# Layer 1 of a four-layer fused kernel: the order of work inside a step, the place of the next sample's gather, and the expert biases

## The reference, cut to what matters

```python
xn = _layernorm(x, axis=-1)
# s: causal scores of 32-wide queries and keys, softmax, values
V = inputs @ (Wvdown @ Wvup);  s = softmax(masked(Q @ K.T / sqrt(32))) @ V
# g: 8 experts of 128x128, top 1 by the router
logits = xt @ router_w + router_b;  probs = softmax(logits)
gate = max(probs);  idx = argmax(probs)
out_all = einsum('th,ehd->ted', xt, expert_w) + expert_b[None]
y = gate * out_all[t, idx];  x = x + s * silu(y)
```

## Time and profile before

| what | us |
|---|---|
| median of 3 runs | 1436.09 (1435.06 to 1437.58) |
| the profiled execution | 1434.19 |
| its span, first to last instruction | 1432.4 |
| layer 0, ends at | 573.3 of the span |
| layer 1 | 573.3 to 732.8 |
| layers 2 and 3 | 732.8 to 1432.4 |
| PE / DVE / ACT / POOL busy over the span | 82 / 70 / 53 / 42 % |

### The profile page before, as it was taken

How to read it: one execution, slowest core, us unless ns; L and a number is a source line. 1 busy time by engine, 2 the same in 40 slices (tenths; PEclk the granted TensorE clock), 3 DMA queues, 4 the chain that set the end, 5 groups by cost and what they waited for, 6 DMA issues and landing times. The chain is left out here.

```text
span 1432.4 us, 21079 instructions
## 1 busy us (share of the span) xinstructions
PE 1169.7 (82%) x7042; PEld 828.3 (58%) x7042; DVE 999.9 (70%) x2279; ACT 762.1 (53%) x1579; POOL 606.8 (42%) x601
## 2 busy tenths in 40 slices
PE   3999999998888694687876887888887874899995
PEld 1455655664554483476653554656555653678885
DVE  2476677679787464567646988989889896714555
ACT  1456556555445354344436685676677472426553
POOL 3243445444358633533101532724633543315772
PEclk9999999999999897688878998898899797779997
DMA  7300000000000122800000000000000000001113
GB/s 179 109 1 1 1 1 1 1 2 1 1 13 24 57 86 74 268 11 15 1 12 0 1 1 1 1 1 0 1 1 1 0 1 0 30 8 34 45 42 107
DMA packets 54456, 40.72 MB, mean 28 GB/s; under 512 B 13191, under 2 KB 46701, under 8 KB 54349
## 3 DMA queue, kind: packets, MB, share of 16 engines
q1 hardware_dynamic: 41006, 27.58, 6.6%
q0 software_dynamic: 4544, 9.32, 2.3%
q10 hardware_dynamic: 8800, 2.48, 0.9%
HBM read 26.32 MB, written 13.04 MB: 27 GB/s over the span
## 5 line engine op out<-in xcount | busy, mean ns | idle before, releaser
L780 POOL TENSOR_TENSOR PR<-PR,R 128x512 f32<-128x512 f32 (+3 forms) x128 | 160.5, 1266 | 230.3 <-DVE R L1260 229.8
L1978 POOL TENSOR_TENSOR YY<-YY,H 128x512 f32<-128x512 f32 x120 | 162.3, 1375 | 206.3 <-DVE H L2349 206.3
L410 PE MATMUL banks<-XT,we 128*128 128x128 f32 (+1 forms) x568 | 178.1, 445 | 11.2 <-ACT HH L2196 10.8
L1067 ACT ACTIVATE PR<-banks,NM 128x257 f32<-128x257 f32 (+3 forms) x256 | 132.4, 527 | 99.3 <-DVE NM L1232 97.5
L410 PEld LDWEIGHTS banks<-we,HH 128*128 128x128 f32 x1024 | 147.5, 208 | 36.6 <-issue 32.1
L2341 DVE TENSOR_TENSOR_SCAN H<-DA,H 128x1024 f32<-128x1024 f32 x64 | 164.6, 2572 | 0.4 <-DVE OH L466 0.3
L410 PE MATMUL banks<-we,HH 128*128 128x128 f32 x1024 | 147.5, 292 | 0.0
L2196 ACT ACTIVATE HH<-banks,be1f 128x512 f32<-128x512 f32 x128 | 84.1, 686 | 93.1 <-PE banks L410 92.4
L410 PEld LDWEIGHTS banks<-XT,we 128*128 128x128 f32 x568 | 91.2, 203 | 65.3 <-issue 44.2
L410 PE MATMUL banks<-BCR,SEL 96*128 96x512 f32 x128 | 68.9, 540 | 72.5 <-DVE H L2349 61.2
L410 PEld LDWEIGHTS banks<-PTS,V 128*64 128x64 f32 x1152 | 65.9, 138 | 86.0 <-issue 50.2
(11 more groups left out here) (535 smaller groups left out, 2461.1 us busy)
## 6 DMA issues: line engine op xcount, KB each, us to landing
xsort<-zrow SPq DMA_DIRECT2D x1, 3072.0 KB, 13.8
XS<-xsort SPq DMA_DIRECT2D x12, 256.0 KB, 3.0
ysort<-PTS SPq DMA_DIRECT2D x12, 256.0 KB, 2.2
pj_stage<-in_L_ffn_w_proj SPq DMA_DIRECT2D x1, 2048.0 KB, 11.9
we<-in_L_ffn_we SPq DMA_DIRECT2D x1, 2048.0 KB, 15.1
we<-yrows SPq DMA_DIRECT2D x8, 256.0 KB, 4.5
xrows<-XN SPq DMA_DIRECT2D x4, 256.0 KB, 2.3
out<-XN SPq DMA_DIRECT2D x4, 256.0 KB, 2.3
```

Of the source, the lines that this page charges most:

```text
L410: return nc.tensor.matmul(o, l, r, start=start, stop=stop)
L780: last = nc.gpsimd.tensor_tensor(p, p, R[:, T * q + t, :].unsqueeze(2).to_broadcast([P, 2, w]), ALU.mult)
L1067: nc.scalar.activation(PR0[:, q % 2, s, OFF[t]:OFF[t] + w], ps2(n)[:, s, SLOT[t]:SLOT[t] + w], ACT.Exp, bias=NM[:, m, s:s + 1], accum_out= ...
L1978: nc.gpsimd.tensor_tensor(YY[:, m, :], YY[:, m, :] if n else XD[m], H[:, k % 4, m, :], ALU.add).then_inc(ya, 1)
```

## The change

1. **The biases are folded.** Two small loads put the 8 bias rows of layer 1's experts into partition 0 of XN and SA, which are free during layer 0. In three free slots of the spare bank in layer 0's last sample (u = 9, 10, 11) PE forms the column sums of the expert weights less the bias, and of the query, key, value and router weights; DVE subtracts a 128th part of them from the weights. In layer 1 ACT stores the features with 1 added. As normed rows sum to zero, features plus one times the new weights is the old product plus bias. The weights transpose, its store, the bias products and `store_bias` go, and the first expert is written into ACC by a multiplication instead of added.
2. **The steps are turned round.** Sample j + 1 is weighed after the last row maximum of step j, its gate is stored and its norm statistics are taken after expert 5, its norm applied between experts 6 and 7. A step therefore begins on PE with the features of sample j, then expert 0, transposes 0, queries and keys, logits, expert 1, and so on. ACT's order follows.
3. **Gathers a step ahead.** POOL issues the gathers of sample j + 2 at the end of step j, behind the inverse deviation of sample j + 1.

```diff
-                    return ("sel",) if u == 8 else None
+                    return {8: ("sel",), 9: ("e1", 0), 10: ("e1", 1), 11: ("q1",)}.get(u)
...
+                            elif kind == "e1":
+                                pe.wait_ge(s_late, 16)
+                                mm(o, ones[:, :], EW[:, 4 * b:4 * b + 4, :].rearrange("p e d -> p (e d)"), start=True, stop=False)
+                                last = mm(o, minus[0:1, :], (XN, SA)[b][0:1, :, :].rearrange("p t d -> p (t d)"), start=False, stop=True)
+                            elif kind == "q1":
+                                for i, w in enumerate((wqp, wkp, wv1, Wr1)):
+                                    last = mm(o[:, i * P:i * P + w.shape[1]], ones[:, :], w[:, :])
...
+                                w = EW[:, 4 * b:4 * b + 4, :].rearrange("p e d -> p (e d)")
+                                nc.vector.scalar_tensor_tensor(w, o, -1.0 / P, w, ALU.mult, ALU.add).then_inc(m7, 1)
...
POOL, layer 1
+                        scales(0)
+                        gather_rows(g, 1, YG, s_back[1])
+                        for j in range(B):
                             for t in range(T):
                                 g.wait_ge(fi, T * j + t + 1)
                                 nc.gpsimd.tensor_tensor(SC[:, j % 2, t, :], SC[:, j % 2, t, :], FI[:, t % 2, :], ALU.add).then_inc(fd, 1)
+                            if j + 1 < B:
+                                scales(j + 1)
+                            if j + 2 < B:
+                                g.wait_ge(ya, j + 1)
+                                gather_rows(g, j + 2, YG, s_back[j + 2])
...
ACT
-                            nc.scalar.activation(XT[:, j % 2, :], PS[:, 0, :], ACT.Copy).then_inc(xts, 1)
+                            nc.scalar.activation(XT[:, j % 2, :], PS[:, 0, :], ACT.Identity, bias=ones[:, 0:1]).then_inc(xts, 1)
```

More of the change, by code:

```diff
@@ L1524, in expert @@
                             last.then_inc(yp, 1)
[L1526 to L1534, removed]
-                        def biases(b):
-                            pe.wait_ge(wTs, b + 1)
-                            weighted_biases(0, NE, Eb).then_inc(bi, 1)
                         def transposes(b, t):
@@ L1579, in _ @@
                             front, back, more = j < B, j > 0, j + 1 < B
+                            if front:
+                                features(j)
                             if back:
-                                weights(b)
                                 expert(b, 0)
+                                transposes(b, 0)
+                            if front:
+                                queries_keys(j)
+                                logits(j)
+                            if back:
                                 expert(b, 1)
                                 turn(TURNS[j][0:1])
-                                transposes(b, 0)
-                                biases(b)
                                 transposes(b, 1)
                             if front:
-                                features(j)
+                                scores(j, 0)
+                                scores(j, 1)
                             if back:
@@ L1593, in _ @@
                                 values(b, 1)
-                                turn(TURNS[j][1:2])
                             if front:
-                                queries_keys(j)
-                                logits(j)
+                                v_rows(j)
+                                scores(j, 2)
                             if back:
                                 expert(b, 3)
+                                turn(TURNS[j][1:2])
                                 transposes(b, 2)
@@ L1602, in _ @@
                             if front:
-                                scores(j, 0)
-                                scores(j, 1)
+                                scores(j, 3)
+                            if more:
+                                choices(j + 1)
                             if back:
@@ L1608, in _ @@
                                 values(b, 2)
-                                values(b, 3)
-                            if front:
-                                v_rows(j)
-                                scores(j, 2)
-                            if back:
-                                expert(b, 5)
-                            if more:
-                                choices(j + 1)
-                            if front:
-                                scores(j, 3)
-                            if back:
-                                expert(b, 6)
-                                turn(TURNS[j][3:4])
                             if more:
@@ L1624, in _ @@
                             if back:
+                                values(b, 3)
+                                expert(b, 5)
+                                turn(TURNS[j][3:4])
+                                expert(b, 6)
+                                turn(TURNS[j][4:])
                                 expert(b, 7)
-                                turn(TURNS[j][4:])
                     @block.scalar
@@ L1833, in _ @@
                             if front:
[L1834 removed]
+                                router(j)
                             if back:
                                 add_expert(b, 1)
[L1837 to L1841 removed]
                             if front:
@@ L1863, in _ @@
                             if back:
-                                add_expert(b, 7)
+                                add_expert(b, 4)
+                                add_expert(b, 5)
                             if more:
                                 finish_next(j + 1)
+                                stats_in(j + 1)
+                            if front:
+                                choose(j)
                             if back:
+                                add_expert(b, 6)
+                            if more:
+                                apply_in(j + 1)
+                            if back:
+                                add_expert(b, 7)
                                 finish(b)
```

102 lines of the change are left out of this document (45 added, 57 removed).

## The result

The changed kernel takes **1415.5 us** (median of 4 runs, 1412.72 to 1425.31) where the kernel before took 1435.8 on the same chip (4 runs, 1435.06 to 1437.58): a ratio of 0.9866, 95% interval 0.9836 to 0.9895. The forecast was 1425.4 with a range from 1417 to 1433, so the gain of 20 us is nearly twice the 10.7 forecast. On a second chip the ratio was 0.9872 (0.9843 to 0.9901), 18.6 us of 1451.9, so the size is no accident of one chip.

A forecast was written before the change was run, and what follows sets the result against it. A chain from engine to engine was taken to bound layer 1's steps, with bias waits and PE's low clock. From 1434.19 us, -11.4 + 0.7 gave 1423.5; with 1.9 for the median, 1425.4, range 1417 to 1433.

The forecast's parts named there:

- Layer 1: The new order and folding end this layer at 721.4 us instead of 732.8, 11.4 us earlier.
- The middle step: Layer 1, from one sample's features to the next: 34.3 us by a walk of the new order, against 37.5 before.
- DVE's waits: In a middle step of layer 1 they sum to 6.2 us, against 10.4 before, with none for ACC.
- Rival (a): Layer 1's PE pause is only moved and DVE's waits stay at 10.4 us: 9.6 us lost, 1435.0 us; chance 0.10.
- Layer 0: The folding's added PE and DVE work in the last sample, mostly covered by POOL's queue: +0.7 us, bounds 0 and 7.4.
- Rival (c): The folding costs its full 7.4 us in layer 0, reads holding up key and query products: 1432.1 us; chance 0.11.
- The gathers: Layer 1's gathers, issued a step ahead on POOL, end before the first fill with 3.2 us slack: 0, bounds 0 and 2.
- The clock in layer 1: PE runs at half clock for the first 5.6 us of a step, after idling over 5 us.
- rival (b): Half clock lasts through the head of layer 1's steps: 4.6 us more in each of steps 1 to 3, 1439.2; chance 0.07.
- Rival (d): Layer 1's waits for scores 3 and the silu shrink: steps of 31.5 us, 1417 us in all; chance 0.08.
- the sum: Whole kernel: -11.4 us for layer 1 and +0.7 for layer 0 give -10.7; no term for layers 2 and 3.
- the signs that the prediction named as proof against it: Steps longer than 36 us, a second fall of the clock, or fills that wait for gathers.

The follow-up runs named there:

- experiment 1: The kernel before with only the biases folded, ratio 0.9941, or only the new step order, ratio 0.9953.
- experiment 2: The changed kernel without its three folding jobs in layer 0's last sample: ratio 0.9903, layer 0 ending at 576.35 us.
- experiment 3: The changed kernel with useless PE products behind expert 7 in layer 1: six 0.9919, eight 0.9921, eight in steps 1 and 2 only 0.9892.
- experiment 5: DVE multiplications added at layer 1's end: changed kernel with 3, 8, 16: 0.9911, 0.9956, 0.9983; kernel before with 16: 1.0061.
- experiment 6: Useless PE products in layer 2's pauses: two everywhere, changed kernel 0.9931, before 0.9991; chosen places, before 0.9906, changed with layer 1's products 0.9834.
- experiment 4: Both kernels run again unchanged on a second chip: changed kernel 0.9872, kernel before against itself 0.9986.

## Why the prediction missed

**Layer 1: right.** Features at 603.11, 637.78 and 672.22 us, forecast 603.35, 637.65 and 671.95; the end at 720.5, forecast 721.4. The middle step, forecast as 34.3 us, took 34.4 to 34.7. Of DVE's waits, forecast as 6.2 us (gate 0.7, logits 2.1, scores 1.9, silu 1.5), 7.2 were measured: 0.7, 1.9, 2.4 and 1.8, and 0.4 for an expert that the forecast had without a wait. The gain of 11.8 us, 12.6 on the second chip, stands against a forecast of 11.4. The last stretch was 1.1 us shorter than forecast (48.3, not 49.4). Over all profiles the kernel before took 157.5 us for this layer on the mean of five, the changed code 146.0 on the mean of eight without products in it: 11.5 us. Rival (a) is out: the pause has indeed stayed (7.09 us), but the waits have shrunk.

**The parts.** The prediction priced a middle step with both parts only, and that price was right. Taken apart, the folding frees the first step (3.1 to 5.1 us); what it does alone in a middle step is not shown (experiment 1).

**Layer 0: right in kind.** Forecast +0.7 us, measured -0.45 and -0.9, with 3.3 us more of PE's work (4.1 forecast); under cover, as argued, and less than this layer's spread of 6 us between executions. Rival (c), 7.4 us, is out by the means of experiment 2.

**The gathers: right, and the change was none.** Before, too, the gathers of a sample stood between the inverse deviation of the sample ahead of it and that sample's fills, so POOL's order in time is the same; they begin at 601.85 us where they began at 604.43. The one row maximum that waits for a fill, 0.6 us in step 0, does so in both kernels; the term of 0 stands.

**The clock in layer 1: right in kind.** Half speed for 5.1, 4.6 and 4.2 us from the start of steps 1 to 3, forecast as 5.6, and no second fall behind it in these steps, against rival (b). The Trainium skill ("TensorE: Matmul & The Clock Gate", Why this matters for your kernels) names pauses between bursts as what costs the clock. With eight products in the pause the clock stayed at 1.00, which agrees. The price is 0.4 to 1.1 us a fall (experiment 3), not the 2 us and more that PE loses.

**Rival (d): its time without its mechanism.** It gave 1417 us by steps of 31.5 us. The time came out near it, but no step was under 33.7: what is missing from the forecast lies in layers 2 and 3, and the closeness is accident.

**Where it failed: the sum ended with layer 1.** "-11.4 + 0.7 = -10.7 us" holds layers 1 and 0 and nothing else; it took the times of layers 2 and 3 from the profiled execution of the kernel before as constants, since their code does not change, and names neither a term nor a reason for that. They brought 3.8 and 5.3 us in the profiled execution. Layer 2's part, about 4 us in both pairs, goes with its earlier start (experiment 5) and comes from falls of PE's clock across products that DVE waits for; filled pauses make the two layers equal (experiment 6). Layer 3's part is chance: its three long waits were 10.6, 7.8 and 10.9 us before and 6.9, 6.6 and 9.3 after in the first pair, and just the other way round in the second; in the three later pairs of experiments 5 and 6 layer 3 gains 2.8, -0.7 and 0.1 us. Of the medians' 20.3 us, 12.3 are thus layers 0 and 1 by the profiled pair, about 4 layer 2, and some 4 are not accounted for; the interval is as wide (4 us either way). None of the signs that the prediction named as proof against it appeared, since all of them look at layers 0 and 1. The range should have held a term of both signs for this: the same layer 2 has taken 479.6 to 486.4 us, and the trace of the kernel before shows a clock of 0.87 and 0.88 in these layers, so that there was something to lose or win.

## What to carry to other kernels

A part of a kernel that isn't edited is not a constant if PE pauses in it: look at its granted clock, and where it is under 1 at products that another engine waits for, give the forecast a term of both signs (layer 2 spread by 6.8 of 483 us here, some 0.7% either way). Such a part is worth an experiment of its own: useless products in the pauses, left out wherever PE's next product is already late, gave this kernel 12 to 14 us in a layer that no reordering had touched. And a low clock costs what the chain loses, not what PE loses: at the start of a step of layer 1 PE lost about 2 us (4 at half speed) and the layer 0.4 to 1.1, while in layer 2 the products took 3.2 us longer, and DVE waited 3.2 us longer for them.

## What was unexpected of the hardware

- **The clock falls after some pauses and not after others of the same length.** After 2.43 us it fell from 1.00 to 0.50 about a microsecond behind PE's new start in one execution, after 2.44 us at the same place of another kernel it did not (experiment 4). With a pause of 1.94 us it still fell (experiment 3), with 0.23 us it did not. The Trainium skill ("TensorE: Matmul & The Clock Gate", What's actually happening) says that the same kernel meets different numbers of slow products in different runs, and puts the penalty of the ramp at under 1% of a typical span. The first agrees with these traces; the second holds only just, as layer 2 alone lost 12 to 14 of 1432 us, and what the other layers lost was not measured.
- **One code's layer 1 does not always take the same time.** The kernel before took 36.9 to 38.1 us for nine of ten middle steps in five executions, and 34.9 for one. In seven of the ten the clock fell a second time right behind the features, in this one it did not. That isn't the whole reason: of the two others without a second fall one took 37.2 us at the same clock of 0.90, one 37.1 at 0.85, and in these ACT waited 5.6 us, and DVE 6.8, for something that the profile calls remote. The changed kernel took 33.7 to 34.7 us for all of sixteen in eight executions, and in none of them did the clock fall a second time.
- **Layer 3 takes 211 to 216 us on three chips and 223 to 231 on three others**, the kernel before and the changed one alike. On the slower ones the profile puts 29 to 33 us of DVE's waits in it, up to 3.6 each, down to something remote; on the faster ones there is no such wait. DVE's idle time there is 110 to 118 us, against 97 to 102. The same chips, and only they, show such waits in layer 1 (up to 6.8 us each, 2.6 to 13.9 in all), and none in layers 0 and 2. What it is stays open. It cancels in the ratios of layer 3's times, but it blurs the steps of layer 1 where profiles of different chips are compared.
